# Records in token order, the tokens of each expert's slots by one-hot products, and expert rows gathered by index

## What is computed

```python
x = x + tanh(g_xattn) * xattn(layernorm(x), ctx, ctx, W_qkv, b_qkv, W_out, b_out)
x = x + tanh(g_ffn) * moe(layernorm(x), Wg, W1, b1, W2, b2)
# in moe, T = 4096 tokens, E = 8 experts, C = 512 slots each, F = 512:
idx = argmax(softmax(tokens @ Wg))
locations1 = cumsum(one_hot(idx)) - 1            # order of arrival at the expert
mask1 = one_hot(idx) * (locations1 < C)          # the 513th and later get nothing
hidden = relu(expert_in @ W1 + b1)
out = gate * (hidden @ W2 + b2)                  # back at the token's place
```

## Time and profile before

| | |
|---|---|
| median of 3 runs | 315.67 us (314.27 to 316.78) |
| the profiled execution: own time | 313.11 us |
| its span (first to last instruction) | 311.3 us |
| TensorE busy, share of the span | 245.3 us, 79% |
| VectorE | 208.0 us, 67% |
| ScalarE | 150.1 us, 48% |
| GpSimd | 181.8 us, 58% |
| 16 DMA engines, moved | 39.25 MB, 126 GB/s |
| TensorE's mean granted clock | 0.902 of 2.4 GHz |

### The profile page before, as it was taken

How to read it: one execution, slowest core, us unless ns; L and a number is a source line. 1 busy time by engine, 2 the same in 40 slices (tenths; PEclk the granted TensorE clock), 3 DMA queues, 4 the chain that set the end, 5 groups by cost and what they waited for, 6 DMA issues and landing times. The chain is left out here.

```text
span 311.3 us, 8092 instructions
## 1 busy us (share of the span) xinstructions
PE 245.3 (79%) x2864; PEld 157.6 (51%) x2864; DVE 208.0 (67%) x718; ACT 150.1 (48%) x347; POOL 181.8 (58%) x235
## 2 busy tenths in 40 slices
PE   1748989699999779879879798896106999999940
PEld 0425736446647546546546455553003577777730
DVE  4676668579999799799779969963300455555610
ACT  4452776477776766766765545572001422222100
POOL 6626928409839949949949907447750055555671
PEclk9998579899999999999999959996555999999985
DMA  4653846924726506616405511147216255554310
GB/s 114 176 153 99 238 144 204 277 72 107 221 56 188 163 31 167 181 35 185 135 29 154 158 34 41 55 133 170 73 47 168 69 169 172 165 169 126 98 51 15
DMA packets 50919, 39.25 MB, mean 126 GB/s; under 512 B 9698, under 2 KB 47223, under 8 KB 50880
## 3 DMA queue, kind: packets, MB, share of 16 engines
q1 hardware_dynamic: 47168, 28.67, 33.8%
q0 software_dynamic: 3712, 10.07, 9.9%
HBM read 13.72 MB, written 12.65 MB: 85 GB/s over the span
## 5 line engine op out<-in xcount | busy, mean ns | idle before, releaser
L645 ACT ACTIVATE prob<-TS 128x512 f32<-128x512 f32 x128 | 72.1, 590 | 49.5 <-PE TS L480 47.8
L759 DVE TENSOR_REDUCE negm<-S 128x4 f32<-128x512 f32 x128 | 82.0, 683 | 15.6 <-PE S L465 13.9
L496 PE MATMUL O<-prob,vals 128*32 128x128 f32 x1024 | 56.2, 295 | 3.7 <-ACT oraw L654 3.6
L1154 POOL DMA_INDIRECT out_dram<-fin,tok x32 | 31.6, 988 | 11.5 <-issue 9.9
L1081 POOL DMA_INDIRECT rec_dram<-rec,slot x32 | 32.3, 1009 | 10.1 <-issue 6.4
L496 PEld LDWEIGHTS O<-prob,vals 128*32 128x32 f32 x1024 | 21.3, 111 | 26.4 <-issue 10.9
L260 POOL TENSOR_TENSOR rest_k<-full_k,parts_k 128x512 f32<-128x512 f32 x7 | 8.0, 1147 | 45.2 <-ACT parts_k L628 45.2
L465 PE MATMUL S<-kp,qp 62*128 62x128 bf16 x512 | 31.8, 231 | 1.3 <-DVE negm L759 1.0
L480 PE MATMUL TS<-qp,kp 64*128 64x128 bf16 x512 | 29.2, 227 | 3.3 <-DMA qp<-mrow 3.2
L593 PE MATMUL X<-w2s,qp 128*128 128x128 f32 x256 | 29.7, 275 | 0.0
L593 PEld LDWEIGHTS X<-w2s,qp 128*128 128x128 f32 x256 | 29.2, 192 | 0.5 <-issue 0.5
(11 more groups left out here) (134 smaller groups left out, 485.8 us busy)
## 6 DMA issues: line engine op xcount, KB each, us to landing
kp<-parts_k SPq DMA_DIRECT2D x48, 128.0 KB, 2.5
qp<-parts_q SPq DMA_DIRECT2D x48, 128.0 KB, 2.6
rec_dram<-zeros POOLq DMA_DIRECT2D x8, 516.0 KB, 5.5
xr<-rec_dram SPq DMA_DIRECT2D x8, 260.0 KB, 3.7
x_sb<-in_x_dram SPq DMA_DIRECT2D x8, 256.0 KB, 4.0
c_sb<-in_ctx_dram SPq DMA_DIRECT2D x8, 256.0 KB, 3.9
out_dram<-rec SPq DMA_DIRECT2D x8, 256.0 KB, 2.7
w1s<-in_L_ffn_W_dram SPq DMA_DIRECT2D x8, 256.0 KB, 3.9
```

What stands on the lines that cost most here:

```text
L496: mm = nc.tensor.matmul(o_out[i * HV:(i + 1) * HV, u * L:(u + 1) * L], vals[G % 2][:, k, h, :], prob[n % 2][:, h * L:(h + 1) * L], start=( ...
L645: nc.scalar.activation(prob[n % 2][:, first:first + 4 * L], TS[:, a, :], ACT.Exp).then_inc(a_exp, 1)
L759: V.tensor_reduce(negm[n % 2][:, first:first + 4], S[:, a, :].rearrange("p (h k) -> p h k", k=L), AX.X, ALU.max, negate=True).then_inc(v_r ...
L1154: G_.indirect_dma_start(out_rows, bass.IndirectOffsetOnAxis(tok[p][:, t:t + 1], 0), fin[p][:, t, :], None, bounds_check=T - 1, oob_is_err= ...
```

## The change

Records are now written in the order of the tokens, one plain transfer a group (SyncE, at j = 3, four batches at once), and the experts' rows are fetched from there by index. No zero fills are needed. The index lists come from products: for each token VectorE forms a one-hot row of its place in a tile of 128 slots (`one_r`, 128x512) and a one-hot of the tile (`one_c`, 32 columns for 8 experts of 4 tiles) multiplied by the token's batch and by its partition (`coded`); TensorE multiplies the two (task `idx`, four products of 128x64 a group), and VectorE adds the result to `holder` (`held`). At the end `tokens_of_slots` makes two lists: the row to read (0 for an empty slot) and the row to write (out of bounds for one).

The second normalisation is ScalarE's (four activations of 128x128 right behind the logits' exponential), with scale and bias from GpSimd (`statistics2`), and GpSimd scales the logits' differences ahead, at j = 0. In the expert stage the plain loads `xe` and `xr` are replaced by GpSimd's indirect gathers of whole records of 264 numbers into one of four buffers `gx`, four gathers an expert. The first four experts' gathers are issued at once, and those of expert e+4 behind the scatters of expert e. Four products of `w1s` by the identity, whose result is not used, stand ahead of the first transposes. The constants come in two transfers.

```diff
-REC = 2 * P + 2
+REC = 2 * P + 8
...
-        xe = [sb(f"xe{i}", [P, ET, D]) for i in range(2)]
-        xr = [sb(f"xr{i}", [P, ET, REC - D]) for i in range(2)]
+        gx = [sb(f"gx{i}", [P, ET, REC]) for i in range(4)]
...
+                if j == 3 and is_group(g - 2):
+                    sp.wait_ge(a_xn2, g - 1)
+                    sp.wait_ge(v_gate, g - 1)
+                    sp.dma_start(rec_v[:, bass.ds((g - 2) * GB, GB), :], rec[(g - 2) % 3][:]).then_inc(rec_out[(g - 2) % 3], 16)
...
-            for p in range(3):
-                sp.wait_ge(sent[p], zeros_sent(p) + 16 * GB * len(range(p, NG, 3)))
-            for e in range(2):
-                load_xe(e)
-            for e in range(2):
-                load_xr(e)
-            sp.wait_ge(p_eT, 1)
-            load_xe(2)
...
+                elif name == "idx":
+                    pe.wait_ge(v_one, idx + 1)
+                    pe.wait_ge(v_coded, idx + 1)
+                    for k in range(GB):
+                        mm = nc.tensor.matmul(X[:, 1, 0:2 * COLS], one_r[:, k, :], coded[:, k, :, :].rearrange("p i c -> p (i c)"),
+                                              start=(k == 0), stop=(k == GB - 1))
+                    mm.then_inc(p_idx, 1)
...
+            pe.wait_ge(w1_in[0], 16)
+            pe.wait_ge(v_red, 4 * B)
+            for _ in range(4):
+                nc.tensor.matmul(S[:, 1, :], ident, w1s[0][:], start=True, stop=True)
...
+                    act.wait_ge(g_nm2, G + 1)
+                    for k in range(GB):
+                        mm = nc.scalar.activation(rec[G % 3][:, k, 0:D], rec[G % 3][:, k, D:2 * D], ACT.Identity,
+                                                  bias=nm2[:, k:k + 1], scale=rs2[:, 1, k:k + 1])
+                    mm.then_inc(a_xn2, 1)
...
+                spread = [P, GB, COLS]
                 dve.wait_ge(v_pos, G + 1)
+                V.tensor_reduce(loc[:], at_e[:], AX.X, ALU.add).then_inc(v_place, 1)
+                done(1)
+                V.tensor_tensor(passed[:], loc[:].unsqueeze(2).broadcast_to(spread), steps, ALU.is_ge).then_inc(v_place, 1)
+                done(2)
+                V.tensor_reduce(tile[:], passed[:], AX.X, ALU.add).then_inc(v_place, 1)
+                done(3)
+                V.scalar_tensor_tensor(row[:], tile[:], -float(P), loc[:], ALU.mult, ALU.add).then_inc(v_row, 1)
+                V.scalar_tensor_tensor(col[:], choice[:], float(ET), tile[:], ALU.mult, ALU.add).then_inc(v_place, 1)
+                done(4)
+                V.tensor_tensor(one_c[:], iota_c, col[:].unsqueeze(2).broadcast_to(spread), ALU.is_equal).then_inc(v_place, 1)
+                done(5)
+                if G >= 1:
+                    dve.wait_ge(p_idx, G)
+                V.tensor_tensor(coded[:, :, 0, :], one_c[:], iota_p[:, G * GB + 1:G * GB + GB + 1].unsqueeze(2).broadcast_to(spread),
+                                ALU.mult)
+                V.tensor_scalar(coded[:, :, 1, :], one_c[:], own, None, ALU.mult).then_inc(v_coded, 1)
+                dve.wait_ge(v_row, G + 1)
+                V.tensor_tensor(one_r[:], iota_p.unsqueeze(1).broadcast_to([P, GB, P]),
+                                row[:].unsqueeze(2).broadcast_to([P, GB, P]), ALU.is_equal).then_inc(v_one, 1)
                 dve.wait_ge(a_lexp, G + 1)
-                V.tensor_reduce(loc[:], at_e[:], AX.X, ALU.add)
                 V.tensor_reduce(lsum[:], lexp[:], AX.X, ALU.add).then_inc(v_place, 1)
-                V.tensor_copy(rec[G % 3][:, :, 2 * D + 1], token_code[:, bass.ds(G * GB, GB)])
-                done(1)
-                V.tensor_scalar(over[:], loc[:], float(CAP), float(NONE), ALU.is_ge, ALU.mult)
-                V.scalar_tensor_tensor(base[:], choice[:], float(CAP), loc[:], ALU.mult, ALU.add).then_inc(v_place, 1)
-
-                V.reciprocal(rec[G % 3][:, :, 2 * D], lsum[:])
-                done(2)
-                V.tensor_tensor(slot[G % 3][:], base[:], over[:], ALU.add).then_inc(v_slot, 1)
+                done(6)
+                V.reciprocal(rec[G % 3][:, :, 2 * D], lsum[:]).then_inc(v_gate, 1)
+
+            def held(G):
+
+                dve.wait_ge(p_idx, G + 1)
+                if G >= 1:
+                    dve.wait_ge(v_idx, G)
+                V.tensor_tensor(holder[:], X[:, 1, 0:2 * COLS], holder[:], ALU.add).then_inc(v_idx, 1)
+
+            def tokens_of_slots():
+
+                dve.wait_ge(v_idx, NG)
+                V.scalar_tensor_tensor(found[:], holder[:, 0:COLS], float(P), holder[:, COLS:], ALU.mult, ALU.add).then_inc(v_found, 1)
+                dve.wait_ge(v_found, 1)
+                V.tensor_scalar(from_row[:], found[:], -float(P), 0.0, ALU.add, ALU.max).then_inc(v_from, 1)
+                V.tensor_scalar(nobody[:], found[:], 1.0, float(NONE), ALU.is_lt, ALU.mult).then_inc(v_found, 1)
+                dve.wait_ge(v_found, 2)
+                V.scalar_tensor_tensor(to_row[:], found[:], -float(P), nobody[:], ALU.add, ALU.add).then_inc(v_to, 1)
...
+                if j == 0 and is_group(g - 3):
+                    held(g - 3)
...
-            def norm2(G):
-
-                to, spread = rec[G % 3][:, :, 0:D], [P, GB, D]
+            def statistics2(G):
+
                 if G >= 1:
+                    pool.wait_ge(a_xn2, G)
                     pool.wait_ge(g_ldif, G)
+                pool.wait_ge(v_mv2, G + 1)
+                G_.tensor_tensor(neg2[:], mv2[:, :, 0], pool_c[:, 2, :], ALU.mult).then_inc(g_neg2, 1)
                 root(G, mv2, rs2, v_mv2, g_e2).then_inc(g_rs2, 1)
-                G_.tensor_tensor(to, rec[G % 3][:, :, D:2 * D], mv2[:, :, 0:1].broadcast_to(spread), ALU.subtract).then_inc(g_sub2, 1)
+                pool.wait_ge(g_neg2, G + 1)
                 pool.wait_ge(g_rs2, G + 1)
-                pool.wait_ge(g_sub2, G + 1)
-                G_.tensor_tensor(to, to, rs2[:, 1, :].unsqueeze(2).broadcast_to(spread), ALU.mult).then_inc(g_xn2, 1)
-
-            def scatter(G, k):
-                p = G % 3
-                if k == 0:
-                    if G == 0:
-                        for q in range(3):
-                            pool.wait_ge(sent[q], zeros_sent(q))
-                    pool.wait_ge(g_xn2, G + 1)
-                    pool.wait_ge(v_slot, G + 1)
-                    if G == NG - 1:
-                        pool.wait_ge(g_fence, NG - 1)
-                    fence()
-                G_.indirect_dma_start(rec_dram, bass.IndirectOffsetOnAxis(slot[p][:, k:k + 1], 0), rec[p][:, k, 0:REC], None,
-                                      bounds_check=T - 1, oob_is_err=False).then_inc(sent[p], 16)
+                G_.tensor_tensor(nm2[:], neg2[:], rs2[:, 1, :], ALU.mult).then_inc(g_nm2, 1)
...
+            def rows_in(e):
+
+                if e >= 4:
+                    pool.wait_ge(v_res, e - 3)
+                    pool.wait_ge(p_eT, e - 3)
+                for t in range(ET):
+                    G_.indirect_dma_start(gx[e % 4][:, t, :], None, rec_dram,
+                                          bass.IndirectOffsetOnAxis(from_row[:, e * ET + t:e * ET + t + 1], 0),
+                                          bounds_check=T - 1, oob_is_err=False).then_inc(first_in[t] if e == 0 else gx_in[e % 4], 16)
...
+            for p in range(3):
+                pool.wait_ge(rec_out[p], 16 * len(range(p, NG, 3)))
+            pool.wait_ge(v_from, 1)
+            fence()
+            for e in range(4):
+                rows_in(e)
             for p in range(3):
                 pool.wait_ge(x1_out[p], 16 * len(range(p, NG, 3)))
+            pool.wait_ge(v_to, 1)
             for e in range(E):
                 for h in range(2):
                     rows_out(e, h)
+                if e + 4 < E:
+                    rows_in(e + 4)
...
```

158 lines of the change are left out of this document (80 added, 78 removed).

## The result

The changed kernel takes 328.93 us (median), the kernel before 316.23 us beside it: a ratio of 1.040, 95% interval 1.031 to 1.049. It is slower. The profiled execution of the changed kernel has an own time of 326.78 us and a span of 324.2, against 313.11 and 311.3 before. The difference of the two, 13.7 us, is to be explained.

A forecast was written before the change was run, and what follows sets the result against it. Each stage has its own limit: VectorE in the loop, TensorE in the expert stage, there GpSimd's queue after the change. 313.1 + 6.8 (T) + 11.9 (experts) = 331.8, put at 333; range 318 to 343.

The forecast's parts named there:

- The expert stage: GpSimd's queue of 32 gathers and 32 scatters, 1.28 us each, ends the stage at T+97.9 against T+86.0: +11.9 us.
- T: End of the last residual addition, 219.12 us in the kernel before; forecast to move by 6.8 us, to 225.9.
- the four unused products: Warming products ahead of the first transposes, at T+5 to T+10: no gain counted, at most first products of 2.08 us halve.
- The transition: From last residual to first gather: records written from T+5.0, landing in 4.7 us, fence and gap 0.71; first gather at T+10.6.
- The loop: Attention loop: -5.0 fills, +6.5 VectorE net, +3.8 ScalarE, sum +5.3 us; with +1.5 in the pipeline's emptying, T moves 6.8.
- The fills: Eight zero fills of the loop: dropping them removes waits around an mrow transfer at 57.73, 5.0 us, bounds 0 and 6.
- `place`: VectorE's eleven instructions a group where seven were, 2.70 us against 0.60: +2.2 us a group, +13.3 over six groups.
- ScalarE's delay: Four normalisations a group behind lexp make mrow 1.2 to 1.4 us late in groups 0, 4 and 5: +3.8 us.
- The term of the blocked copies: Loop: VectorE's four-element copy (L881), held by GpSimd, takes 1.95 us instead of 0.17; removing the excess gains 6.8 us.
- 1, cheap gathers: Expert stage: gathers cost about 0.78 us, TensorE binds again, total 319, as a median 320; chance 0.14.
- 2, the loop gives back what the experts lose: Loop: added VectorE and ScalarE work falls into idle time, T moves by -11.8, total 313.2; chance 0.10.
- 3, holds on the new operations: Loop: GpSimd's addition holds new VectorE operations, each of six groups loses 1.8 us, +10.8, total 343; chance 0.08.

The follow-up runs named there:

- plain_all: Changed kernel with all 32 gathers replaced by plain SyncE transfers of consecutive rows, so experts work on wrong tokens; 309.06 us, ratio to before 0.987.
- plain_late: Changed kernel with only the 16 gathers of experts 4 to 7 replaced by plain SyncE transfers of consecutive rows; 316.73 us, ratio to before 1.008.
- no_warm: Changed kernel without the four unused products of w1s by the identity ahead of the first transposes; 335.51 us, ratio to before 1.070.
- fills_back: Changed kernel with the eight zero fills added back in GpSimd's queue, into a spare buffer nobody reads; 347.69 us, ratio to before 1.106.
- norm_by_act: Kernel before with only the second normalisation moved to ScalarE and the logits' differences scaled ahead; 315.0 us, ratio 1.003.
- add_late: Kernel before with GpSimd's 128x544 addition at j = 3 instead of j = 2; 317.64 us, ratio 1.004.
- one_r_thrice: Changed kernel with the one_r comparison done three times a group, two of them into spare buffers; 350.16 us, median of two.
- code_by_reduce: Kernel before with the four-element copy of the tokens' codes done by a tensor_reduce; 316.28 us, ratio 1.011.
- unheld: Kernel before with second normalisation on ScalarE, fills issued by SyncE, token-code copy as tensor_reduce, slot comparison as scalar_tensor_tensor; 303.83 us, ratio to before 0.965.

## Why the prediction was right, and which term was off

**The expert stage** decided, as forecast, and step by step. Forecast: spacing 1.28, last scatter at T + 97.9, +11.9 us. Measured: 1.30, T + 97.8, +11.8. plain_all and plain_late show that it is the number of indirect transfers. Two things in it were not forecast. What the gathers cost against no gathers is 17.6 us; 5.8 of it are given back by the early plain part of the change. And the stage ends some 9 us later in kernels whose first results come 1.7 to 2.9 us later (no_warm, fills_back), through a cycle of GpSimd's queue and TensorE's as far as the rows tell. That the changed kernel was spared this was luck: the prediction did not look at it. It counted no gain for the four unused products, at most that the first products halve; leaving them out costs 6.6 us, though the first products take 2.07 us with them or without.

**The transition** was 1.0 us dear. I took 4.7 us for the landing of the records, the row says 2.98; against that, the transfer started at T + 5.6, not T + 5.0, and fence and gap took 0.86, not 0.71. The first gather started at T + 9.6, not T + 10.6 (the forecast's own terms add up to T + 10.4). The Trainium skill, DMA: Bandwidth & Descriptors, Anatomy of one DMA, gave an estimate of 3.2 us; its fit is for transfers that GpSimd issues, and this one is SyncE's, but the trace's 2.98 lies near it. The fence's 0.71 is its price where GpSimd had been idle; between transfers it costs 0.37 (263.59 to 263.96). That saved some 2.5 us over the stage, and GpSimd's waits for the first and some late results took them again.

**The loop** is the term that was off in size: T was to move by 6.8 us and moved by 1.7 in the profiled pair (2.0 to 4.2 in the other five executions). By marks of the profiled pair:

| stretch | forecast | measured |
|---|---|---|
| up to mark 2 (no fills) | -5.0 | -6.8 |
| mark 2 to 3 (place of group 0) | +3.5 | +2.2 |
| mark 3 to 6 (groups 1 to 3) | +1.2 | -0.2 |
| mark 6 to 7 (group 4) | +2.0 | +1.7 |
| mark 7 to T (groups 5, 6) | +5.0 | +4.9 |

The fills took 6.8 us here and 3.3 to 6.6 in the other five executions, so the 5.0 lies inside the scatter; what I summed were the waits of one place, 57 to 64 us, and the spacing from mark 1 to mark 2 alone fell by 4.4. `place` and ScalarE's delay were over-sized together, by 1.3 us in group 0, 1.4 in groups 1 to 3 and 0.3 in group 4. I added the two, but VectorE's wait for `mrow` is now 1.02 us in each of the six groups, where I had 1.2 to 1.4 more in three of them and no change in groups 1 to 3, in which it was 1.42 to 1.55 before. The term of the blocked copies, -6.8, took a held time for a loss. It can't be checked alone: the groups 1 to 3, in which it was to pay for most of `place`, came out within 0.6 us of the forecast each, and in norm_by_act a hold 1.0 shorter went with a spacing 1.0 to 1.2 shorter; but in add_late another wait took the hold's place and nothing was gained. Which of the two a kernel gets, no run here separates.

**The rivals.** 1, cheap gathers, falls with the spacing of 1.30. 2, the loop gives back what the experts lose, is the one with most truth in it: the loop took 5 us less than forecast; but one_r_thrice, 18 us slower or more in all for 1.2 us of work a group, shows that VectorE's work is not hidden. 3, holds on the new operations, falls: GpSimd's addition ended 3.1 us ahead of `place`. The Trainium skill, SBUF — State Buffer, Who interferes with whom, would have held them had they overlapped, and the trace agrees in the other kernels: tensor_scalar 1.85 us in code_by_reduce, scalar_tensor_tensor with two SBUF inputs 0.82 in unheld, and no hold on a reduce.

The range of 318 to 343 held the median of 328.93, which lies 4.1 under the 333 forecast: T gave 5.1 less, and the median lies 2.2 above its profiled execution where I had put 1.2.
